# The first pair's norm, router and up products move from the head of the second phase into the last two passes of the first

## The reference, cut to what matters

```
x = x + delta_rule_attention(layernorm(x))     # gated recurrence over each sequence, 16 value heads
x = x + swiglu_like_moe(layernorm(x))          # router, 8 experts of 176 hidden, 1 shared expert
x = x + rotary_attention_and_mlp(layernorm(x)) # 16 heads of 8, then a gelu MLP
x = x + gelu_moe(layernorm(x))                 # router, 8 experts of 512 hidden, 1 shared expert
```

```
def _expert(x, w1, b1, w3, b3, w2, b2):
    h = jax.nn.silu((x @ w1 + b1) * (x @ w3 + b3))
    return h @ w2 + b2
scores = jax.nn.softmax(xf @ gate_w.T, axis=-1)
```

## Time and profile before

| what | value |
|---|---|
| median of the 3 runs shown | 1583.46 us (1576.72 to 1585.36) |
| the profiled execution's own time | 1569.76 us |
| its span, first to last instruction | 1567.9 us |
| mean granted TensorE clock | 0.878 of full speed |
| PE busy | 1321.6 us (84%) |
| DVE busy | 911.5 us (58%) |
| ACT busy | 726.7 us (46%) |
| POOL busy | 194.2 us (12%) |

### The profile page before, as it was taken

The page is one execution under the profiler, slowest core; times in us unless marked ns, Lnnn a source line. Parts: engine busy times, 40 slices in busy tenths (PEclk is TensorE's granted clock), DMA queues, the critical chain, the costliest instruction groups (busy, mean ns, idle before and its releaser), DMA issues.

```text
span 1567.9 us, 26862 instructions
## 1 busy us (share of the span) xinstructions
PE 1321.6 (84%) x11048; PEld 956.3 (61%) x11048; DVE 911.5 (58%) x2365; ACT 726.7 (46%) x1353; POOL 194.2 (12%) x186
## 2 busy tenths in 40 slices
PE   2759889798979979887859786989899988989899
PEld 2345767566666756656846453676566655676567
DVE  4696878979697897968134623463344524354321
ACT  1547465664746566472414143523444344533442
POOL 5011121212122121212020001000000001000000
PEclk9768869798896978887679777999999999999999
DMA  3000000000000000000210000000000000000000
GB/s 120 4 1 4 1 2 11 2 11 2 11 1 2 11 2 8 2 30 2 84 75 1 8 1 0 0 8 1 1 8 1 8 1 7 1 1 1 2 7 8
DMA packets 15066, 17.69 MB, mean 11 GB/s; under 512 B 2567, under 2 KB 13216, under 8 KB 14560
## 3 DMA queue, kind: packets, MB, share of 16 engines
q1 hardware_dynamic: 12768, 14.09, 2.7%
q0 software_dynamic: 576, 1.76, 0.3%
q10 hardware_dynamic: 1600, 0.12, 0.1%
HBM read 13.87 MB, written 2.10 MB: 10 GB/s over the span
## 4 chain that ended last, share of the span: by engine, by line
PE 60%; DVE 25%; ACT 9%; issue 3%; POOL 1%; DMA 1%; SPq 0%; DVEq 0%; ACTq 0%
PE ps L1405 8%; PE ps L1395 8%; PE ps L1354 6%; PE ps L1036 5%; DVE arena L1746 4%; DVE arena L1749 4%; PE ps L1018 4%; DVE arena L1990 2%; ACT arena L900 2%; PE ps L1497 2%; PE ps L1094 2%; PE ps L1461 2%; PE ps L1074 2%; PE ps L1003 1%; PE ps L1184 1%
## 5 line engine op out<-in xcount | busy, mean ns | idle before, releaser
L1664 DVE SCALAR_TENSOR_TENSOR arena<-ps,conv_w,arena 128x255 f32<-128x255 f32 (+2 forms) x384 | 163.8, 475 | 19.4 <-ACT arena L609 14.9
L853 ACT ACTIVATE arena<-ps 128x512 f32<-128x512 f32 x144 | 85.2, 597 | 180.7 <-PE ps L1395 180.6
L1405 PEld LDWEIGHTS ps<-arena 128*128 128x128 f32 x1152 | 132.6, 192 | 24.8 <-issue 9.9
L1405 PE MATMUL ps<-arena 128*128 128x128 f32 x1152 | 136.9, 277 | 7.1 <-ACT arena L853 4.1
L1395 PE MATMUL ps<-arena 128*128 128x512 f32 x288 | 134.3, 612 | 0.0
L516 POOL TENSOR_TENSOR rstd<-var_eps,half_power 128x2 f32<-128x2 f32 (+1 forms) x28 | 23.3, 832 | 650.9 <-DVE var_eps L1635 650.9
L1911 DVE SCALAR_TENSOR_TENSOR arena<-ps,gates,arena 128x128 f32<-128x128 f32 x128 | 36.0, 343 | 114.0 <-PE ps L1405 113.7
L1036 PE MATMUL ps<-arena 64*128 64x256 f32 x256 | 82.9, 462 | 16.1 <-ACT arena L618 16.1
L1732 DVE TENSOR_TENSOR arena<-ps,arena 128x512 f32<-128x512 f32 x64 | 44.1, 689 | 81.9 <-PE ps L1036 70.5
L2027 DVE TENSOR_REDUCE arena<-ps 128x8 f32<-128x2048 f32 (+1 forms) x24 | 54.9, 2292 | 62.2 <-PE ps L1461 62.2
L1036 PEld LDWEIGHTS ps<-arena 64*128 64x128 f32 x256 | 52.4, 220 | 62.0 <-DVE arena L1734 24.1
(11 more groups left out here) (246 smaller groups left out, 2904.0 us busy)
## 6 DMA issues: line engine op xcount, KB each, us to landing
arena<-in_routed_up SPq DMA_DIRECT2D x1, 2048.0 KB, 9.6
arena<-in_routed_down SPq DMA_DIRECT2D x1, 2048.0 KB, 15.0
x_ln<-in_x SPq DMA_DIRECT2D x8, 128.0 KB, 2.2
arena<-in_w_mix SPq DMA_DIRECT2D x1, 1024.0 KB, 11.0
x_in<-in_x SPq DMA_DIRECT2D x8, 128.0 KB, 2.4
out_x<-x_res SPq DMA_DIRECT2D x8, 128.0 KB, 1.9
arena<-out_x SPq DMA_DIRECT2D x4, 256.0 KB, 2.7
out_x<-arena SPq DMA_DIRECT2D x4, 256.0 KB, 2.2
```

What stands on the lines that cost most here:

```text
L853: act.activation(hid1[half][:, i, :], ps[:, banks[i], :], ACT.Gelu).then_inc(s["mgelu"], 1)
L1405: mm = pe.matmul(ps[:, bank, c * P:(c + 1) * P], hid1[half][:, i, c * P:(c + 1) * P], m_down[:, e, i, :], start=(i == 0), stop=(i == HT1 - 1))
L1664: ins = dve.scalar_tensor_tensor(conv_tile(f, m)[:, sh:SEQ], ps[:, PAIR_BANK[p], j * SEQ:(j + 1) * SEQ - sh], conv_w[:, m, TAPS - 1 - sh:T ...
```

## The change

Pair 0's head is taken apart and put between the steps of passes 6 and 7.

- SP loads `pair_in` for pair 0 in pass 6 as soon as the outputs of sequence 6 are done; the first pair consists of sequences 0 and 1, which were stored long before.
- VectorE runs `first_norm(0)` at the end of pass 6, with GpSimd's power between; TensorE turns it after `solve64`, ScalarE copies it to `hT0`.
- Router logits and up tiles 0 to 4 go between `solve_and_merge64`, `merge64` and `turn_heads(6, 1)` in pass 6; tiles 5 to 13 go between the steps of the chunk chain of sequence 7. The router's softmax and choice (`route`, about 20 small VectorE instructions) stands behind `sum_squares(7, 0)`.
- Because phase 1 still uses banks 4 to 7, pair 0's tiles get only two bank pairs (`2 * (k % 2)`), so a tile waits for the product of tile `k - 2`, and one `prod` buffer, so the product of an even tile waits for the Silu of the two tiles before it. `gate3` has three buffers in place of four.
- Several tiles move in memory, so that the new ones lie beside what phase 1 still holds. Pairs 1 to 3 compute in the old order.

```diff
+def up_bank(p, k):
+    return 2 * (k % (3 if p > 0 else 2))
+def prod_of(p, k):
+    return (k // 2) % 2 if p > 0 else 0
...
+                if it == SEQS - 2:
+                    sp.wait_ge(s["o_psum"], 4 * (SEQS - 1))
+                    sp.wait_ge(s["x1_stored"], 16 * 2)
+                    sp.dma_start(pair_in[:, :, :], pair(out, 0)).then_inc(s["pair_loaded"], 16)
...
-            sp.dma_start(pair_in[:, :, :], pair(out, 0)).then_inc(s["pair_loaded"], 16)
...
+            def up_tile(p, k):
+                if p == 0 and k >= 2:
+                    pe.wait_ge(s["prod_ready"], k - 1)
+                elif p > 0 and k >= 3:
+                    pe.wait_ge(s["prod_ready"], p * UP0 + k - 2)
...
+                i = UP_ORDER[k]
+                for j, w in enumerate((w1, w3)):
+                    mm = pe.matmul(ps[:, up_bank(p, k) + j, :], w[:, i * P:(i + 1) * P], hT0[:, :], start=True, stop=True)
+                mm.then_inc(s["up_psum"], 1)
...
                 if has_n:
                     merge64(n, 0)
+                if it == SEQS - 2:
+                    up_tile(0, 2)
+                if has_n:
                     merge64(n, 1)
+                if it == SEQS - 2:
+                    up_tile(0, 3)
...
             project_out(SEQS - 1, SEQS, 1, False)
+            up_tile(0, 13)
...
-                pe.wait_ge(s["w_b_in"], 16 * 10)
-                pe.wait_ge(s["w1_in"], 16)
-                pe.wait_ge(s["hT_ready"], it * N_HT + 1)
-                route(hT0, gate_w[:, :])
-                for k, i in enumerate(UP_ORDER):
...
+                if it > 0:
+                    route_first(it)
+                    for k in range(UP0):
+                        up_tile(it, k)
+                else:
+                    pe.wait_ge(s["x_updated"], CH * SEQS)
...
+            def product_of_tile(p, k):
+                dve.wait_ge(s["gate_done"], p * UP0 + k + 1)
+                if k % 2 == 0 and k >= (4 if p > 0 else 2):
+                    dve.wait_ge(s["hid_ready"], p * UP0 // 2 + k // 2 - (1 if p > 0 else 0))
```

More of the change, by code:

```diff
@@ L237, in program @@
         pad = sb("pad", [P, 1])
-        dm = [carve(1, [HEADS, P]) for _ in range(2)]
+        dm.append(carve(1, [HEADS, P]))
         um = carve(1, [HEADS, P])
@@ L270, in program @@
         hid0 = carve(2, [UP0, G * P])
[L271 to L276, removed]
+        gate3 = [carve(2, [G * P]) for _ in range(3)]
+        prod = [carve(2, [2, G * P])]
+        pair_in = carve(2, [G, P])
+        prod.append(carve(2, [2, G * P]))
+        qk_tok = carve(2, [G * 2, AH, AP], at=AT_PAIR).rearrange("p (c q) h d -> p c q h d", q=2)
+        qT = carve(2, [AG, G * P], at=AT_PAIR + G * 2 * AH * AP)
+        kT = carve(2, [AG, G * P], at=AT_PAIR + G * 2 * AH * AP + AG * G * P)
         probsT = [carve(2, [4, 512]) for _ in range(2)]
@@ L763, in _ @@
                     squares(i, 0)
+                if it == SEQS - 1:
+                    hidden_tiles_of(0, 5)
+                    gate_of_tile(0, 6)
+                    gate_of_tile(0, 7)
+                    router(0, 0)
+                if has_i:
                     solutions(i, 1)
+                if it == SEQS - 1:
+                    hidden_tiles_of(0, 7)
                 if has_n:
@@ L925, in pair_layers @@
                 transpose_out(3)
-                router(1)
+                router(it, 1)
                 for e in range(FIRST_LATE if more else EXPERTS):
@@ L1317, in _ @@
                     turn_heads(i, n, 1, 1, has_n)
+                if it == SEQS - 2:
+                    up_tile(0, 4)
+                if it == SEQS - 1:
+                    up_tile(0, 12)
             project_out(SEQS - 1, SEQS, 1, False)
-            def turn_first(i):
-                pe.wait_ge(s["h_ready"], i * N_LN + 1)
-                for c in range(G):
-                    mm = pe.transpose(ps[:, 7, c * P:(c + 1) * P], h_tok[:, c, :], ident)
-                mm.then_inc(s["hT_psum"], 1)
+            up_tile(0, 13)
             def pair_layers(it, more):
@@ L1881, in _ @@
                     normalise(i, 1)
+                if it == SEQS - 2:
+                    first_norm(me, 0, 0)
+                    first_norm(me, 0, 1)
+                    dve.wait_ge(s["w_b_in"], 16 * 10)
+                    for k in range(5):
+                        product_of_tile(0, k)
+                if it == SEQS - 1:
+                    product_of_tile(0, 12)
                 if has_f:
@@ L1885, in _ @@
             residual(SEQS - 1, 1)
-            def first_norm(me, i, part):
-                if part == 0:
-                    dve.wait_ge(s["pair_loaded"], 16 * i + 16)
-                    norm_before(me, pair_in, NORMS[0], "")
-                else:
-                    norm_after(me, pair_in, h_tok, NORMS[0], "", i * N_LN + 1)
+            product_of_tile(0, 13)
             me2 = Steps(dve, s["dve_step2"], 0, 0)
@@ L1966, in pair_layers @@
-                dve.wait_ge(s["w_b_in"], 16 * 10)
-                route(0, True)
-                for k, i in enumerate(UP_ORDER):
-                    dve.wait_ge(s["gate_done"], it * UP0 + k + 1)
-                    if k >= 4 and k % 2 == 0:
-                        dve.wait_ge(s["hid_ready"], it * UP0 // 2 + k // 2 - 1)
-                    dve.scalar_tensor_tensor(prod[(k // 2) % 2][:, k % 2, :], ps[:, 2 * (k % 3), :], b1[:, i:i + 1],
-                                             gate3[k % 4], ALU.add, ALU.mult).then_inc(s["prod_ready"], 1)
+                if it > 0:
+                    route(me, it, 0, True)
+                    for k in range(UP0):
+                        product_of_tile(it, k)
```

258 lines of the change are left out of this document (178 added, 80 removed).

## The result

| | before | after | ratio (95% interval) |
|---|---|---|---|
| median, all runs of this comparison | 1581.33 us (1576.72 to 1585.36) | 1540.55 us (1537.97 to 1544.43) | 0.9745 (0.9709 to 0.9782) |
| profiled execution | 1569.76 us | 1541.31 us | |
| its span | 1567.9 us | 1539.5 us | |
| mean granted clock | 0.878 | 0.89 | |

(With a fourth run before's median is 1581.33 us, not the 1583.46 of the three runs shown earlier.) Between the two profiled executions the gain is 28.4 us. So there are two questions: why those two differ by more than 24.1, and where the other 12 us of the medians come from.

The account below looks back on a forecast made before the run. Bound: the serial seam from 808.4 to 848.7, 40.3 us. Lags of 8.7 (pass 6) and 7.5 (pass 7), together 16.2, leave 24.1 us less: 1583.5 - 24.1 = 1559 us; own range 1551 to 1567, 8 in 10 1546 to 1575.

Parts of the forecast that it names:

- the two waits that were forecast: TensorE in pass 7: 0.5 us at sequence 7's second-chunk outputs, behind the router; 2.8 us at the last scaling.
- the rival in which the clock falls in pass 7: Tiles 8 to 13 at low clock cost 10.3 us more; gain 14 us, 1569 us; chance 0.13.
- the prediction's own signs of being wrong: PE gaps over 1 us at sequence 7's outputs or solves, low clock between 776 and 830, or pass 6's turn awaiting `h_tok`.
- the quoted rule: Trainium skill: TensorE idling briefly between matmul groups while cycling PSUM banks can swing clocks; prediction countered with 772.9 to 800.2 staying high.
- slower: Half clock until the down products: 34 us against the gain of 24, so 10 us slower, 1593 us; chance 0.04.
- nothing filled: Tiles in passes 6 and 7 leave old gaps: lag 24.9 us, gain 15 us, 1568 us; chance 0.06.
- ScalarE and VectorE on the path: Gates, products and Silus, 27.5 us; over nine tenths of it on the path leaves no gain, 1583 us; chance 0.05.
- I assume the offset stays.: The median of before's runs shown stood 13.7 us above its profiled execution; the forecast kept this for the changed kernel.
- the lag of pass 6: Pass 6 ends 8.7 us later: 14.8 us of added work less filled gaps, 3.4, and earlier clock rise, 1.0 and 1.7.
- my bounds of 766 to 776: Pass 6: the granted clock rises at about 769, between 766 and 776, worth plus or minus 1.7 us.
- The reason given for the rise: Pass 6: tile 0 brings long dense matmuls from about 760.6, and the clock rises at about 769 in place of 772.9.
- in case the offset is one of the day: Why the 8-in-10 range reached down to 1546 us, the profiled execution's forecast time.

Follow-up runs that it names:

- after_again: The changed kernel, unchanged, run again on a second chip beside the kernel before: 1541.47 us, ratio 0.9801.
- before_again: The kernel before, unchanged, with its own profiled execution: median 1572.59 us, ratio 0.9995; profiled execution 1572.93 us.
- before_look2: A further copy of the kernel before, unchanged, profiled once on a third chip: 1583.0 us.
- set 2: Runs on a second chip: the changed kernel again, two edits of it, and dummy matmuls in the kernel before, whose unedited median there was 1573.96 us.
- scale_first: Against the changed kernel: scaling of the last chunk ahead of product 11 on VectorE, tile 12 ahead of the turned heads on TensorE; 1534.79 us, ratio 0.977.
- router_early: Against scale_first: ScalarE's router exponential ahead of solutions(7, 0), VectorE's route behind residual(6, 1); 1535.2 us, ratio 0.9704 to the kernel before.
- tiles_0_4: Against the changed kernel: tiles 0 to 4 stay in pass 6, tiles 5 to 13 go behind the last projection; 1555.02 us, ratio 0.989 to before.
- head_only: Against the changed kernel: load, norm, turn and logits stay early, all fourteen up tiles go behind the last projection; 1560.08 us, ratio 0.9917 to before.
- late_slots: Against the changed kernel: only tile 0 in pass 6, tiles 1 to 9 in pass 7, tiles 10 to 13 behind the last projection; 1542.02 us, ratio 0.9795.
- filler_levels: The changed kernel plus six unread 128x128 by 128x512 matmuls before solve32(7, 0) in pass 6; 1544.68 us, ratio 0.983 to the kernel before.
- set 3: Runs on a third chip: three more copies of the kernel before, and router_early; the median of the kernel before there was 1582.56 us.
- the fillers: The kernel before plus unread matmuls: four before the last turned heads, nine before turn_first(0); median 1572.12 us, ratio 0.9993.

## Why the prediction was wrong, point by point

**The mechanism of the move was right.** The seam is closed; tile 13 is the only one behind the last projection; the logits, the router and the tiles cause the two waits that were forecast (0.45 for 0.5, 2.70 for 2.8); the router's turn starts at 822.84 for 824.6. Pass 7 cost 8.0 us more than before (`residual(6, 1)` to tile 13's end, less 36.0), forecast 7.5, and the difference is tile 12 at half clock, 1.5 us, less what the other steps gained. That fall is the only trace of the rival in which the clock falls in pass 7, and one of the prediction's own signs of being wrong, a low stretch between 776 and 830; it came behind the wait that was named for it, lasted 3.4 us, not to the end of the tiles, and was absent in after_again. The row set against the quoted rule was weaker than it reads: before's clock fell at 800.2 inside the gap of 4.59 us that ended at 801.97, so that stretch did not outlast its widest gap. Nothing of "slower", "nothing filled" or "ScalarE and VectorE on the path" is to be seen. The weights of phase 2 and the norm were in time.

**The step that failed: "I assume the offset stays."** The sum was made on the profile of a short execution of before, 1569.76 us, and carried to the median by adding 13.7 us to both kernels. The offset is no constant of the measurement: in before_again it was 0.3 us. It goes with the time at half clock, and in the longer executions that were traced a part of it lies in the very stage that the change rebuilds: 6.6 us of 13.3 in before_look2, 4.8 in before_again. The changed kernel's median lies 0.8 us below its own profiled execution, and its eight runs scatter over 6 us where the twelve of before_again scatter over 18. The miss in the gain, 40.8 less 24.1 = 16.7 us, consists of

- 11.6 + 0.8 us: before's median lay 11.6 above its profiled execution, after's 0.8 below its own;
- 3.2 us in the stage (next point);
- 2.5 us behind the router's turn (719.2 to 716.7) less 1.4 ahead of the first mark, both in code that did not change; after_again has 719.2 again.

How much of the first term belongs to the stage is not shown, since none of the first comparison's four executions of before was profiled; in before_look2, as long as they were, it was about half. The rest is not the change's doing as far as any trace shows: in set 2, where before's median lay 7.4 us lower, the gain was 32 us.

**A term mis-sized: the lag of pass 6.** Forecast 8.7 us, measured 5.0 (35.1 for 30.15 us from the first mark to `residual(6, 1)`) and 3.2 in after_again. The clock rose at about 765, outside my bounds of 766 to 776, so tile 1 cost 1.91 us, not 3.43, and tile 0 some 0.1 less; tiles 2 and 3 took 1.91 in place of 1.72, which gives 0.4 back. That is 1.2 us. And I had held the 64x64 merges fixed, taking them to be too small to follow the clock; the sum has no term for them. They follow it. Before, 755.7 to 766, and after, 757.3 to 774.2 (groups: count, busy us, mean ns):

```profile
L1100 PE MATMUL ps<-arena 64*64 64x64 f32 x64 | 7.6, 314 | 0.6 <-ACT arena L680 0.6
```

```profile
L1166 PE MATMUL ps<-arena 64*64 64x64 f32 x64 | 5.4, 244 | 0.0
```

That is 2.2 us; the mean of 244 ns still holds sixteen of the 64 at about 310 ns, the others took about 220. With the 1.2 it makes 3.4 of the 3.7 us between 8.7 and 5.0.

The reason given for the rise, the dense matmuls of tile 0, does not hold either. In after_again, scale_first, router_early, tiles_0_4, head_only and late_slots the clock rose 16.7 to 16.9 us after the first mark, behind the turn and ahead of tile 0, and head_only has no tile in pass 6 at all; its logits ran at the high clock:

```profile
758.09 1.11 PE L1300 MATMUL ps<-con,h_tok 128*128 128x128 f32 x4
...
760.96 1.06 PE L1312 MATMUL ps<-gate_w,hT 128*128 128x8 f32 x8
```

The traces of after, with its rise 21 us behind the mark, and of filler_levels, with 24, are the exceptions. In head_only and late_slots, which have no tile between the merges, the clock fell again, at 764.3 and 763.0; with the tiles there it stayed.

**What the range missed.** It was built from doubts about the change (the rise, the waits, the rivals) and took the baseline's doubt on one side only: "in case the offset is one of the day" led down to 1546, the profiled time less the gain. Both the offset's vanishing and a gain of a few us more were needed to reach 1540.55.

**What stays open.** Why the chip of set 3 showed long executions of before in most runs (9 of 10 above 1578 us) and the other two in few (7 of 49); why the same wait of 2.70 us was followed by a fall of the clock in one execution and not in the other; and why the fillers, which held the clock over most of the seam in their one trace, did not narrow the scatter.

## What to carry to other kernels

Where the granted clock of the kernel before changes inside the stage that is edited, take several of its executions before you build a sum on one: the median's distance from the profiled time may be half-clock time that the change removes. Work that fills gaps paid twice here, with the gap and with the clock that stayed high, but tiles moved to where there are few gaps paid little (late_slots). And where a chain hangs on one operation that an engine does last, put it ahead of the independent products on that engine: that gave scale_first, the fastest order here together with router_early, at 1535 us.

## What the hardware showed that I had not expected

- The clock stayed low for 47.7 us while TensorE was busy for 32.3 of them, two thirds (before_look2), and high for 51.2 us at 94% (after). In before it rose at 772.9; with only the turn and the logits put into pass 6 (head_only) it rose first at 760.8, fell at 764.3 and rose again at 774.5.
- It fell at 747.4 among the 32x32 matmuls of the levels, although six matmuls of 128x512 had run until 742.8 and the gap just ahead was 1.18 us (filler_levels). And it stayed high through a wait of 2.70 us (after_again).
- Matmuls of 64x64 shorten with the clock as well: about 310 ns each before the rise, about 220 behind it.
- One unchanged program scatters over 1564.7 to 1585.4 us, with the mean granted clock from 0.882 down to 0.864 in step with it; the changed one, whose stage stays at the high clock, over 1538.0 to 1544.4.
